# Second edge layer of a graph block: product and head sum of a score in one fused instruction per step and head, placed between the two additions of a slot

## What is computed

```python
rel = rel_w[edge_relations]
mod_k = K[src] + 0.2 * rel[:, None, :]
scores = jnp.einsum('ehd,ehd->eh', Q[dst], mod_k) / D ** 0.5
seg_max = jax.ops.segment_max(scores, dst, num_segments=N)
ex = jnp.exp(scores - seg_max[dst])
denom = jax.ops.segment_sum(ex, dst, num_segments=N)
w = ex / denom[dst]
agg = jax.ops.segment_sum(w[:, :, None] * V[src], dst, num_segments=N)
```

## Time and profile before

| | us |
|---|---|
| median of 3 runs (1916.95 to 1919.61) | 1919.19 |
| profiled execution, its own time | 1912.22 |
| its span | 1910.5 |
| VectorE (DVE) busy in the span | 1426.3 (75%) |
| TensorE matmul (PE) busy | 1321.5 (69%) |
| GpSimd (POOL) busy | 1012.8 (53%) |
| ScalarE (ACT) busy | 925.1 (48%) |

### The profile page before, as it was taken

How to read it: one execution, slowest core, us unless ns; L and a number is a source line. 1 busy time by engine, 2 the same in 40 slices (tenths; PEclk the granted TensorE clock), 3 DMA queues, 4 the chain that set the end, 5 groups by cost and what they waited for, 6 DMA issues and landing times. The chain is left out here.

```text
span 1910.5 us, 29161 instructions
## 1 busy us (share of the span) xinstructions
PE 1321.5 (69%) x7038; PEld 919.6 (48%) x7038; DVE 1426.3 (75%) x3659; ACT 925.1 (48%) x3196; POOL 1012.8 (53%) x1082
## 2 busy tenths in 40 slices
PE   5436655665665569998867778777878778563286
PEld 4324433443443457776544555555555554452164
DVE  5458888888988953436868899999999997776043
ACT  2444556555555343322440677777777773231033
POOL 2377777777776000000517777777777775101555
PEclk9767887787777759999986899999999999775599
DMA  5766767667666119000358888888888884325564
GB/s 121 202 175 203 207 200 215 206 207 217 210 208 186 56 30 356 3 1 6 138 199 260 268 265 251 265 261 265 269 261 269 263 266 139 110 69 109 187 192 137
DMA packets 174910, 356.04 MB, mean 186 GB/s; under 512 B 29303, under 2 KB 70825, under 8 KB 174621
## 3 DMA queue, kind: packets, MB, share of 16 engines
q0 software_dynamic: 58192, 175.85, 30.6%
q1 hardware_dynamic: 116558, 178.33, 29.8%
HBM read 268.46 MB, written 89.75 MB: 187 GB/s over the span
## 5 line engine op out<-in xcount | busy, mean ns | idle before, releaser
L796 POOL DMA_INDIRECT e_rows<-h_rows,src_col x416 | 412.9, 993 | 127.0 <-issue 123.6
L1282 POOL DMA_INDIRECT e_rows<-kv_rows,src_col x320 | 306.5, 958 | 99.9 <-issue 66.8
L1042 PE MATMUL e_sum<-e_rows,e_of_dst 128*128 128x264 f32 x832 | 291.1, 489 | 98.3 <-DVE e_rows L887 81.8
L1501 ACT ACTIVATE e_rows<-e_rows 128x64 f32<-128x64 f32 x1152 | 281.4, 335 | 0.3
L1564 PE MATMUL e_query<-q,e_to_dst 128*128 x1248 | 203.5, 294 | 78.3 <-DVE e_rows L1335 58.1
L1042 PEld LDWEIGHTS e_sum<-e_rows,e_of_dst 128*128 128x128 f32 x832 | 172.5, 235 | 141.5 <-DVE e_rows L887 88.9
L1604 PE MATMUL e_sum<-e_rows,e_of_dst 128*128 128x260 f32 x640 | 185.2, 412 | 1.8 <-POOL e_rows L1212 1.2
L1564 PEld LDWEIGHTS e_query<-q,e_to_dst 128*128 128x128 bf16 x1248 | 120.3, 100 | 134.0 <-issue 94.8
L969 ACT ACTIVATE e_rows<-e_rows 128x32 f32<-128x32 f32 x832 | 181.0, 305 | 0.1
L1423 DVE TENSOR_TENSOR acc<-acc,e_sum 128x260 f32 x346 | 145.4, 420 | 41.5 <-DVE acc L1423 20.4
L1282 POOL DMA_INDIRECT x<-kv_rows,src_col x96 | 91.5, 953 | 72.9 <-POOLq L2087 38.5
(11 more groups left out here) (415 smaller groups left out, 2676.0 us busy)
## 6 DMA issues: line engine op xcount, KB each, us to landing
step_of<-e_of_dst SPq DMA_DIRECT2D x104, 256.0 KB, 2.3
e_of_dst<-step_of SPq DMA_DIRECT2D x104, 256.0 KB, 3.7
sorted_rows<-zeros SPq DMA_DIRECT2D x1, 14560.0 KB
rows<-sorted_rows SPq DMA_DIRECT2D x56, 260.0 KB, 2.9
e_rel<-step_rel SPq DMA_DIRECT2D x26, 512.0 KB, 4.3
step_to<-e_to_dst SPq DMA_DIRECT2D x26, 512.0 KB, 5.9
e_to_dst<-step_to SPq DMA_DIRECT2D x52, 256.0 KB, 4.4
e_rows<-h_rows,src_col POOLq DMA_INDIRECT x416, 3.3
```

The source lines that it names most:

```text
L796: pool.indirect_dma_start(out=g[t // BATCH % R][:, t % BATCH, :], out_offset=None, in_=k.h_rows[:, :], in_offset=bass.IndirectOffsetOnAxis ...
L1042: pe.matmul(psm[t % NB], of_dst[q][:, s % GROUP, :], g[m % R][:, s, :], start=True, stop=True).then_inc(summed, 1)
L1282: pool.indirect_dma_start(out=rows_at(t, 1)[:, 0, :], out_offset=None, in_=k.kv_rows[:, :], in_offset=bass.IndirectOffsetOnAxis(ap=k.src_c ...
L1501: ins = act.activation(x, x, ACT.Copy, scale=row[:, plo + h:plo + h + 1])
```

## The change

`score_multiply` and `score_reduce` go. `score_products` takes their place: for each step of the pair and each head, one `tensor_tensor_reduce` over 64 columns that writes the product and puts its sum into one column of `sc2`. It stands in the slot between `add(first)` and `add(first + 1)`. The semaphore `look_used` goes, and TensorE's queries wait for `scored` with the same count. `sc2` gets two buffers; the buffers of `taken` go from 3 to 2.

```diff
-        def score_multiply(m, q):
+        def score_products(m, q):
             v.wait_ge(k.dve_steps, with_relation[m * PAIRS2 + q])
             v.wait_ge(looked, m * PAIRS2 + (q + 1))
-            keys = rows_at(m * LONG + q * QP, QP)[:, :, 0:D]
-            v.tensor_tensor(keys, keys, ps_q[q % 2][:, :, :], ALU.mult).then_inc(look_used, 1)
-
-        def score_reduce(m, q):
-            at = slice(q * QP, (q + 1) * QP)
-            v.wait_ge(look_used, m * PAIRS2 + (q + 1))
-            keys = rows_at(m * LONG + q * QP, QP)[:, :, 0:D]
-            v.tensor_reduce(sc2[:, at, :], keys.rearrange("p s (h f) -> p s h f", h=H), AX_X, ALU.add
-                            ).then_inc(scored, 1)
+            keys = rows_at(m * LONG + q * QP, QP)
+            for t in range(QP):
+                for h in range(H):
+                    head = slice(h * F, (h + 1) * F)
+                    ins = v.tensor_tensor_reduce(
+                        out=keys[:, t, head], in0=keys[:, t, head], in1=ps_q[q % 2][:, t, head], scale=1.0, scalar=0.0,
+                        op0=ALU.mult, op1=ALU.add, accum_out=sc2[m % 2][:, q * QP + t, h:h + 1])
+            ins.then_inc(scored, 1)
...
         for q in range(PAIRS2):
             score_add(0, q)
             if q:
-                score_reduce(0, q - 1)
-            score_multiply(0, q)
+                score_products(0, q - 1)
...
+        score_products(0, PAIRS2 - 1)
...
-                if q == 0:
-                    score_reduce(m, PAIRS2 - 1)
-                elif more:
-                    score_reduce(m + 1, q - 1)
...
-                if more:
-                    score_multiply(m + 1, q)
...
                 elif q == 3:
                     made = maxima(made)
+                if more:
+                    score_products(m + 1, q)
                 add(first + 1, w)
...
-            wait(pe, look_used, pair - 1)
+            wait(pe, scored, pair - 1)
```

More of the change, by code:

```diff
@@ L1119, in edges_second @@
     of_dst = [sb(f"of_dst{q}", [P, GROUP, P]) for q in range(GROUPS)]
-    sc2 = sb("scores2", [P, LONG, H])
+    sc2 = [sb(f"scores2_{b}", [P, LONG, H]) for b in two]
     fwd = sb("fwd", [P, P])
@@ L1142, in edges_second @@
     psm = [b[:, 0:MW] for b in bank]
-    NS = 3
+    NS = 2
     taken = [sb(f"taken{j}", [P, MW]) for j in range(NS)]
@@ L1174, in edges_second @@
     looked = sem("looked")
-    look_used = sem("look_used")
     scored = sem("scored")
@@ L1570, in turn_scores @@
             wait(pe, prob_in_rows, m)
-            pe.transpose(ps_t[:, 0:P], sc2[:, :, :].rearrange("p s h -> p (s h)"), k.ident[:, :]
+            pe.transpose(ps_t[:, 0:P], sc2[m % 2][:, :, :].rearrange("p s h -> p (s h)"), k.ident[:, :]
                          ).then_inc(transposed, 1)
```

## The result

The changed kernel takes **2021.44 us** (median of 4 runs, 2019.07 to 2027.44). The kernel before took 1919.4 us beside it, and the ratio is 1.0532 (95% interval 1.0509 to 1.0554). The span of the profiled execution grew from 1910.5 to 2017.4 us, by 106.9.

A forecast was written before the change was run, and what follows sets the result against it. VectorE was taken to pace the old loop, a circle through TensorE the new one. Terms 162 + 11 + 2 + 5 = 180 us on 1912.2 gave 2092, with 7 us for the median 2099, rounded to 2100 us; range 1980 to 2290.

The forecast's parts named there:

- The closed circle: Main-loop slot: products, TensorE's queries, first sum, addition, products again; 3.75 us a slot against 2.88, +162 us.
- the clock stays near 1: TensorE in the main loop: high clock kept; the rival of a low clock, 2260 us, had 10%.
- GpSimd has time to spare: Main loop: gathers and GpSimd's additions are never late, with almost 1 us to spare a slot.
- P: VectorE's time for a pair's eight fused and eight single-column instructions: 1.7 us, against 1.2 us for the old passes.
- a rival at 1990 us with 8%: VectorE's products: the single column is free, 1.1 us a pair, a slot of 3.15 us, about 1990 us; chance 8%.
- P at 2.9 us as an upper end: VectorE's products: nothing overlaps, 8 x (0.22 + 0.14) = 2.9 us a pair, about 2320 us.
- the rest of the circle: Main-loop slot: the links besides the products, from queries through first sum to the addition's end; 2.05 us.
- slots beyond the circle, and the clock at the start: Main loop: +11 us for slots 3 and 4 of the lots, +5 us for TensorE's low clock at the start.
- The low clock at the start of the loop: TensorE enters the main loop at the low clock, lengthening some six slots; +5 us.
- The extras of a lot: Slots 3 and 4 of a lot: maximum and turn of the probabilities add 0.9 us a lot, 12 lots, +11 us.
- That instructions don't overlap: VectorE's products: 2.3 us a pair gives about 2210 us, 2.9 about 2320; chance 22%, two thirds near 2210.
- That VectorE's own work decides: Main loop: sums come sooner, so VectorE's 3.3 us a slot count; +74 us, about 1990 us; chance 8%.

The follow-up runs named there:

- r3: Changed kernel with its fused products moved back ahead of both additions of the slot, repeated on a faster chip: 1940.41 us, ratio 1.0102 to the kernel before.
- r4: Changed kernel with TensorE making a slot's two sums ahead of the look-ups for the next pair, repeated on a faster chip: 1938.19 us, ratio 1.0095.
- e3: Changed kernel with plain product and reduction passes instead of fused instructions, both between the additions; queries wait for the reduction: 2239.42 us, ratio 1.0376, slower group.
- e6: Changed kernel with sixteen fused instructions of 32 columns instead of eight of 64, half of each score left out: 2495.41 us, ratio 1.1613, slower group.
- e5: Changed kernel with four fused instructions of 128 columns instead of eight of 64, every second head's scores left out: 2164.3 us, ratio 1.0031, slower group.
- e1: Changed kernel with its fused products moved back ahead of both additions of the slot, first run, in a slower group: 2175.68 us, ratio 1.0106.

## Why the prediction came out as it did

**The mechanism was right, and it is shown.** The closed circle (products, queries, sum, addition) sets the loop: its steps stand in the timeline of the changed kernel, and opening it at either of two places (r3, r4) returns 80 of 101 us. The same wait comes with two plain passes (e3). No engine is the bound, the clock stays near 1 (1.00 in the window above), and GpSimd has time to spare, all as forecast.

**The step that failed is the price of the single-column instruction**, P = 8 x (0.14 + 0.07) = 1.70 us. Measured are 1.13. The 0.14 for the fused instruction was right. The 0.07 was taken from an ordinary instruction of one column, but the read of the accumulator starts together with the next fused instruction. That is the case which I had as a rival at 1990 us with 8%. The Trainium skill, VectorE: DVE Perf Modes, section "The DRAIN you can't avoid", has the sentence by which the prediction put P at 2.9 us as an upper end. The same paragraph goes on that "A next op that is not held starts earlier", which the prediction left out, and with that the timeline agrees: each fused instruction starts 0.07 to 0.08 us before the end of the one ahead.

**The other terms of the loop**, 185 slots:

| term | forecast | measured | difference over 185 slots |
|---|---|---|---|
| P | 1.70 us | 1.13 | -105 us |
| the rest of the circle | 2.05 us | 2.14 | +17 us |
| slots beyond the circle, and the clock at the start | 16 us | 28 (what is left) | +12 us |

Together -76 us, and the loop came out at +101.5 where 178 had been forecast. The two small errors happen to make up for 29 us of the large one; with P alone put right the forecast would have been about 1995 us. The rest of the circle was short by one link: from the start of the two sums to the addition it is 0.82 us and not 0.56 + 0.15 = 0.71, since half of a row with four matmuls is not when the second one's result is there: the second of the four ends 0.68 us after the first starts. The low clock at the start of the loop, 5 us in the forecast, cost nothing, since 1.00 was granted from 1057 to 1100 us. The extras of a lot were set at 0.9 us and are 28 / 12 = 2.3: by the medians over the lots, slots 6 to 15 average 3.28 us, which is the circle, and slots 0 to 5, which hold the softmax and its turns through TensorE, 3.60. I had counted only slots 3 and 4.

**The chances.** Of the two cases at 1990 us the one with the free column was right in its cause, and its sum (a slot of 3.15, +68 us) was too low by the same two terms. That instructions don't overlap had 22% and was wrong: fused and read overlap fully, and one fused instruction and the next by 0.07 to 0.08 us. That VectorE's own work decides did not come true, since it waited 108.7 us.

**What the change would have to give, even without the circle,** is in r3: the fused form gains 0.07 us a pair and loses 0.12 where it stands right behind its own keys, and the cover of the short chain besides. This was not in the prediction; P was the only term I had for the form.

What stays open: the causes of what r3 and r4 still lose outside the waits named, the share of the clock in e6, and what holds up every kernel in the two slower groups.

## What to carry to other kernels

Before you move an instruction past another one, write down who is released by it and what stands behind that engine's wait, and go round until you are back or out; if you come back, the period can't be shorter than the sum of the links, however little each engine has to do. Fusing a reduction into a product over short rows is worth the second pass less the additional start-ups: here 0.60 - 7 x 0.075 us, almost nothing, and by e5's distances it would be 0.37 us a pair with four instructions instead of eight. An instruction that stood between a result and its reader was cover, and its removal has a price even where its own time is saved.

## What the runs showed of the hardware

- The read of the accumulator behind a fused product and sum (0.08 us long, 1664 times) adds nothing to the distance between fused instructions: 0.141 us at 64 columns with the read, and 0.14 for a plain instruction of that width.
- Start to start, VectorE's instructions of 32, 64, 128 and 512 columns all lie on 0.075 us and 1.04 ns a column, fused or not. In r3 a reader right behind the writer of its operand, with a semaphore between them, starts 0.12 us later than that (0.72 for 0.60 us).
- TensorE kept the high clock (1.00) in the change's slots of 3.27 us with 66.29 us of 100 busy, and was granted 0.64 in a window of e6, whose slots take 4.97 us, with 64.71 busy. The second busy time has longer matmuls in it, so the two are not the same work.
- The same program took 2155.66 us in one group of runs and 1921.07 in another. Between the profiles of e1 and r3, which are one program, 117 us of the difference lie ahead of the second edge layer, 52 in the 22 pairs and 62 in the loop. A comparison is worth something only beside the kernel before.
